# Linear-attention layer in fp32: the query of the running state as four 32-column tiles per group of features instead of two 64-column tiles

## The reference

```python
xn = _layernorm(x, axis=-1)
q, k, v = jnp.split(xn @ wqkv, 3, axis=-1)          # q, k through relu, then split in 16 heads of 16
kv = jnp.cumsum(k[..., :, None] * v[..., None, :], axis=2)
num = jnp.einsum('bhnd,bhnde->bhne', q, kv)
den = jnp.einsum('bhnd,bhnd->bhn', q, jnp.cumsum(k, axis=2))[..., None] + EPS
y = (num / den) @ wo
x = x + y + ffn(xn)
```

## Time and profile before

| | |
|---|---|
| Median of 3 runs | 1347.9 us |
| Lowest and highest | 1345.97, 1350.45 us |
| Profiled execution, its own time | 1346.54 us |
| Its span, first to last instruction | 1344.8 us |
| Mean granted TensorE clock | 0.997 |
| Busy: TensorE, its weight loads, VectorE | 1313.8, 1136.4, 1114.9 us |
| Busy: ScalarE, GpSimd | 738.3, 814.9 us |

### The profile page before, as it was taken

One profiled execution on the slowest core, in us unless ns is written; L12 is line 12 of the kernel. 1 busy time (PEld: TensorE's weight loads), 2 busy tenths in 40 slices (PEclk: granted clock), 3 DMA queues, 4 the chain that ended last, 5 costly groups with the idle time before them and its releaser, 6 DMA issues.

```text
span 1344.8 us, 54748 instructions
## 1 busy us (share of the span) xinstructions
PE 1313.8 (98%) x24384; PEld 1136.4 (85%) x24384; DVE 1114.9 (83%) x2566; ACT 738.3 (55%) x1545; POOL 814.9 (61%) x679
## 2 busy tenths in 40 slices
PE   4899999999999999999999999999999999999997
PEld 3788888888888888888888888888888888888886
DVE  4888888888888888988888988888888889888885
ACT  4555665555664565654555655555645656545561
POOL 2755666755666656657556666556566566575554
PEclk9999999999999999999999999999999999999999
DMA  4011111111111211111111111121111111111110
GB/s 148 34 66 65 51 48 34 65 65 66 46 53 34 65 65 64 35 45 55 66 65 51 48 35 65 65 65 42 56 35 66 65 65 35 34 65 50 50 49 18
DMA packets 46779, 73.73 MB, mean 55 GB/s; under 512 B 6480, under 2 KB 42192, under 8 KB 42448
## 3 DMA queue, kind: packets, MB, share of 16 engines
q1 hardware_dynamic: 46544, 70.24, 15.1%
HBM read 53.18 MB, written 17.04 MB: 52 GB/s over the span
## 4 chain that ended last, share of the span: by engine, by line
PE 97%; DVE 1%; SPq 1%; ACT 1%; DMA 1%; issue 0%; DVEq 0%
PE ring L300 51%; PE scores L300 17%; PE ring L408 7%; PE ring L422 6%; PE scores L357 5%; PE state_sum L371 4%; PE ring L440 2%; PE scores L310 2%; PE scores L339 2%; DMA x_t<-in_L_attn_x_dram 1%; SPq L257 0%; DVE cT L775 0%; ACT qp L517 0%; DVE sm L753 0%; ACT xn L528 0%
## 5 line engine op out<-in xcount | busy, mean ns | idle before, releaser
L626 POOL TENSOR_TENSOR hid<-hid,cwb 128x512 f32<-128x512 f32 x128 | 169.8, 1327 | 202.6 <-DVE hid L783 200.8
L775 DVE SCALAR_TENSOR_TENSOR cT<-xT,conv_ws,cT 128x512 f32<-128x512 f32 x192 | 288.8, 1543 | 0.0
L614 POOL TENSOR_TENSOR x_t<-x_t,same 128x1024 f32<-128x1024 f32 x32 | 77.1, 2409 | 264.3 <-ACT same L524 264.3
L540 ACT ACTIVATE sg<-ring 128x512 f32<-128x512 f32 x128 | 76.7, 599 | 281.5 <-PE ring L300 281.5
L300 PE MATMUL ring<-xl,wgu_h 128*128 128x512 f32 x512 | 212.0, 414 | 0.0
L300 PE MATMUL ring<-xh,wgu_l 128*128 128x512 f32 x512 | 202.5, 396 | 0.0
L300 PE MATMUL ring<-xh,wgu_h 128*128 128x512 f32 x512 | 201.8, 394 | 0.0
L630 POOL TENSOR_TENSOR hl<-hid,hh 128x512 fp32r<-128x512 f32 x128 | 193.2, 1509 | 0.0
L783 DVE TENSOR_TENSOR hid<-ring,sg 128x512 f32<-128x512 f32 x128 | 88.2, 689 | 110.9 <-PE ring L300 110.9
L480 ACT ACTIVATE yh<-yT 128x256 fp32r<-128x256 f32 x128 | 53.5, 418 | 228.9 <-DVE yT L796 228.9
L753 DVE TENSOR_TENSOR sm<-scores,causal_s 128x512 f32<-128x512 f32 x256 | 158.7, 681 | 20.4 <-PE scores L357 20.2
(11 more groups left out here) (110 smaller groups left out, 3542.6 us busy)
## 6 DMA issues: line engine op xcount, KB each, us to landing
cwb<-cw_rows SPq DMA_DIRECT2D x32, 1024.0 KB, 4.6
x_t<-in_L_attn_x_dram SPq DMA_DIRECT2D x32, 512.0 KB, 4.4
out_dram<-x_t SPq DMA_DIRECT2D x32, 512.0 KB, 2.9
cw_rows<-cwt SPq DMA_DIRECT2D x128, 2.0 KB, 1.4
sm<-in_L_attn_wqkv_dram SPq DMA_DIRECT2D x2, 384.0 KB, 5.5
sm<-in_L_ffn_Wg_dram SPq DMA_DIRECT2D x2, 256.0 KB, 4.2
sm<-in_L_ffn_Wu_dram SPq DMA_DIRECT2D x2, 256.0 KB, 5.8
cwb<-in_L_ffn_Wd_dram SPq DMA_DIRECT2D x1, 512.0 KB, 4.2
```

The lines of the kernel that those rows point to most:

```text
L614: pool.tensor_tensor(xb, xb, same[:, :, :], ALU.add).then_inc(s_base1, 1)
L626: pool.tensor_tensor(hid[:, e, :], hid[:, e, :], cwb[:, e, :], ALU.mult).then_inc(s_hid, 1)
L775: ins = dve.scalar_tensor_tensor(out=cT[:, c, :], in0=xT[:, j % 2, c, n:n + BT], scalar=conv_ws[:, c, n:n + 1], in1=cT[:, c, :], op0=ALU.m ...
```

## The change

The inner loop over two 64-column pieces becomes a loop over four 32-column pieces. `PPG` is 4 and `BLK` is 32. Every piece of 32 columns of `state_bd` is multiplied with the same moving columns of `qT` and goes to its own 32 partitions of the same bank.

```diff
                         for g in range(C):
                             n0 = t * P + h * HALF
-                            for w in range(2):
-
-                                rows = slice(w * HALF, (w + 1) * HALF)
-                                cols = slice(g * P + w * HALF, g * P + (w + 1) * HALF)
+                            for m in range(PPG):
+
+                                rows = slice(BLK * m, BLK * m + BLK)
+                                cols = slice(g * P + BLK * m, g * P + BLK * m + BLK)
                                 ins = mm(NB2[t % 2][h][rows, g * HALF:(g + 1) * HALF], state_bd[:, n % 4, cols],
                                          qT[:, g, n0:n0 + HALF], start=False, stop=True, skip_group_check=True)
```

## The result

The changed kernel took 1369.61 us (median of 4 runs, 1366.15 to 1370.82) where the kernel before took 1346.93 beside it: ratio 1.0162, 95% interval 1.0132 to 1.0192. It is slower by 1.6%, some 22 us; 1344.0 was forecast, and 1341 to 1348.5 as range. The profiled execution, the fastest of the four, has a span of 1364.3 us for 1344.8. All ratios in this document leave out three executions that took much longer than the others of their kernel: 6794 and 1578 us of the kernel before, and 2803 us of the last padded kernel.

The account below looks back on a forecast made before the run. TensorE's own time was taken as the bound, busy 98% of the span. 120 full stages at -31 ns and 8 half stages at -20 gave -3.9 us, from median 1347.9 to 1344.0; range 1341 to 1348.5.

Parts of the forecast that it names:

- The rounds: State query: six further rounds of matmul starts, one per tile, at 55.5 ns for 58.4, saving 17 ns.
- the first gap: State query, first to second round of starts: 80 ns for 107 with half-width weight loads, saving 27 ns.
- the last round: End of the state query: fourth member starts 20 ns behind the first, where the second was 7 behind; costs 13 ns.
- the gaps around the query: Stretches without a start before and behind the state query, 0.146 and 0.152 us, said to stay.
- Rival 1: State query rounds stay at 58.4 ns; -1.8 us in all, 1346.1 us, chance 0.25.
- Issue: 1984 more loads and matmuls pass TensorE's queue: TensorE's queue at the query: 32 records need 365 ns even at the slow pace, under 433; cost taken as 0.
- the -3.9: Forecast net change in us over all state queries: -31 ns in 120 full stages, -20 ns in 8 half stages.
- rival 2: The query's four tiles don't stream side by side; rounds of 91 ns, +22 us, 1370 us, chance 0.09.
- What would show it: Trace signs: rounds of 55 to 58 ns; wrong if over 61, a hole among 32 starts, or neighbouring stages change length.
- Rivals 3 and 4: Gaps around the query shrink, 1312 us, chance 0.06; some 29 ns per start on 128-row tiles, 1405, chance 0.02.

Follow-up runs that it names:

- the last padded kernel: Changed kernel with 136 do-nothing fillers per batch, ahead of head and output products only, plus 22 small matmuls at the start: 1371.42 us, ratio 1.0159.
- the burst: Kernel before with 480 fp32 matmuls of tile 64*32 (1920 instructions) put ahead of everything; these took 29 us, the whole kernel 1397.83 us (one run).

## Why the prediction was wrong

- **The rounds, the first gap, the last round, the gaps around the query:** right, to a few ns. 435 ns for 433, 149 for 152 behind it, and a round takes 56 ns for 58.4 as loads became narrower than streams (55.5 forecast). Rival 1 fell.
- **"Issue: 1984 more loads and matmuls pass TensorE's queue ... I take nothing":** this is the step that failed. It priced how fast the queue hands instructions to the array (6.9 to 11.4 ns each), over the 32 records of one query. It didn't ask how the queue itself is filled. That goes by blocks of 256, each at 3.46 us in the burst and at 2.8 us or more at a hole of the changed kernel, and must be looked at over the whole stretch of work around the change and over the length of a batch. The term is 20 holes, +23.0 us, against the -3.9.
- **"A cover that is gone is rival 2":** rival 2 gave 1370, which is close to 1369.6, but by rounds of 91 ns that are 56. Its chance of 0.09 was for a mechanism that isn't there; the time agrees by accident.
- **"What would show it":** the text looked for holes among the 32 starts or another length of the stages beside the query. The holes are in the scores, one stage further.
- Rivals 3 and 4 fell: both gaps stayed, and starts of the four tiles are 7 ns apart. Against the floor of 25 ns that the Trainium skill gives ("TensorE: Matmul & The Clock Gate", Part 1) the row of the trace was right.
- **What could have been read before:** the row of instruction packets (191, 3.13 MB) together with 352 instructions in 2.9 us at tile 0 and 1533 per batch, 3 short of six blocks. Three numbers, and the change alters all of them. The price of a block was not in that profile.

## What to carry to other kernels

In a kernel that is bound by TensorE and has stretches of small matmuls, count instructions, not only their time: where more than 256 come in under 3.5 us, a border that falls late in the stretch costs about a microsecond, and where a large transfer was under way behind the border before, a hole came even after 4.8 us of work. Such a cost depends on the place of the whole program: 124 instructions ahead of everything brought 2.5% here, and a comparison of two versions should be repeated with one of them shifted by half a block before its verdict is put down to the edit. The waits show it as "issue" on an operation that the edit never touched.

## What the runs showed of the hardware

- TensorE gets its instructions in blocks of 256. In the burst a block takes 3.46 us when the next is wanted at once. From the landing of a packet to its block's first instruction it is 1.2 to 1.6 us at the holes. The Trainium skill, "Advanced Engine Details and Errata", ISA Cache, tells of lines of 256 instructions and "Only 2 cache lines!", though it gives TensorE 128 KB in the same list; the burst, which runs over one border and then stands at every one that follows, agrees with the two.
- A block's packet that comes to start during the program's own 512 KB store starts about when that store ends, 1.5 to 4.0 us behind the border (all 14 holes behind the first batch of the last padded kernel; read from times that agree, not tested).
- The kernel before, shifted by 124 instructions, is 2.5% slower; by 248, the same.
- Four tiles of 128*32 stream side by side at 56 ns per round with 64 columns each in fp32; with a load as wide as the stream (two tiles of 128*64) a round takes 58.4.
